# One-hots of the filled tiles in a two-layer graph network: made by distance and ramp on ScalarE instead of by comparison on VectorE

## What is computed

```python
edge_index = jnp.stack([src, dst])
h = jnp.maximum(_layernorm(x, axis=-1), 0.0)
x = x + _L0_gnn_ref(h, edge_index, W, b)          # xw[src] * norm, summed by dst
h = jnp.maximum(_layernorm(x, axis=-1), 0.0)
x = x + _L1_gnn_ref(h, edge_index, ...)           # attention over the edges:
q = (h[src] @ Wq.T + bq).reshape(-1, 8, 16)
k = (h[dst] @ Wk.T + bk).reshape(-1, 8, 16)
v = (h[dst] @ Wv.T + bv).reshape(-1, 8, 16)
exp_att = jnp.exp(jnp.clip(einsum('ehd,ehd->eh', q, k) / 4, -10, 10))
out = segment_sum(exp_att / segment_sum(exp_att, src)[src] * v, src)
out = layernorm(out + h) * gamma + beta
```

## Time and profile before

| | us |
|---|---|
| median of 3 runs | 2204.95 |
| lowest, highest | 2202.63, 2205.7 |
| the profiled execution, its own time | 2208.58 |
| its span, first to last instruction | 2206.9 |
| granted TensorE clock, mean of the span | 0.886 of full |

### The profile page before, as it was taken

One profiled execution on the slowest core, in us unless ns is written; L12 is line 12 of the kernel. 1 busy time (PEld: TensorE's weight loads), 2 busy tenths in 40 slices (PEclk: granted clock), 3 DMA queues, 4 the chain that ended last, 5 costly groups with the idle time before them and its releaser, 6 DMA issues. The chain is left out here.

```text
span 2206.9 us, 44517 instructions
## 1 busy us (share of the span) xinstructions
PE 1621.2 (73%) x10081; PEld 1279.8 (58%) x10082; DVE 1861.9 (84%) x5001; ACT 1295.7 (59%) x3546; POOL 1495.3 (68%) x1570
## 2 busy tenths in 40 slices
PE   5524355887787787868877778888888888888880
PEld 4424343555554555545556567777777777777770
DVE  9998998967676787676686679999999999999996
ACT  8744446967677767677775544444444444444443
POOL 0067777777777777777773467777777777777756
PEclk8866667988898888989889889999999999999995
DMA  4031221111111111121110744445454454445443
GB/s 140 17 84 52 53 53 51 52 51 52 52 51 52 52 53 52 52 52 51 52 53 14 230 137 137 140 137 142 137 138 142 136 140 139 140 136 140 138 114 58
DMA packets 123938, 202.72 MB, mean 92 GB/s; under 512 B 34205, under 2 KB 85789, under 8 KB 123781
## 3 DMA queue, kind: packets, MB, share of 16 engines
q0 software_dynamic: 59984, 143.85, 23.4%
q1 hardware_dynamic: 54037, 50.75, 8.3%
q10 hardware_dynamic: 9888, 7.80, 1.7%
HBM read 183.20 MB, written 19.08 MB: 92 GB/s over the span
## 5 line engine op out<-in xcount | busy, mean ns | idle before, releaser
L303 POOL DMA_INDIRECT rows<-y_tab,idx x832 | 798.0, 959 | 308.2 <-issue 307.0
L1364 POOL DMA_INDIRECT x<-kv_tab,kv_idx x648 | 625.9, 966 | 263.0 <-issue 179.2
L783 ACT ACTIVATE sort_v<-sort_t,staged,minus 128x128 f16<-128x128 f16 x914 | 360.7, 480 | 115.0 <-PE ps_sort L875 113.3
L622 DVE TENSOR_SCALAR sort_v<-iota_h,staged 128x128 f16<-128x128 f16 x748 | 249.5, 334 | 162.4 <-PE ps_sort L875 161.9
L875 PE MATMUL ps_sort<-sort_hi,sort_v 128*128 128x496 f16 x1662 | 360.2, 374 | 0.1
L833 PE MATMUL ps_sum<-rows,hot 128*128 128x128 f32 x1664 | 254.3, 318 | 139.7 <-DMA rows<-y_tab,idx 97.1
L1614 PE MATMUL ps_kv<-kv_s,hot_low 128*128 x1314 | 325.8, 384 | 31.6 <-DVE hot_low L1388 30.9
L833 PEld LDWEIGHTS ps_sum<-rows,hot 128*128 128x128 f32 x1664 | 246.2, 233 | 152.9 <-issue 75.6
L1601 PE MATMUL ps_m<-msg,x 128*128 128x136 f32 x1728 | 251.6, 288 | 97.3 <-DVE msg L1416 96.7
L1601 PEld LDWEIGHTS ps_m<-msg,x 128*128 128x128 f32 x1728 | 214.5, 189 | 177.4 <-issue 177.4
L775 ACT ACTIVATE sort_t<-iota_h,minus 128x128 f16<-128x128 f16 x831 | 250.9, 387 | 104.1 <-DVE minus L614 104.1
(11 more groups left out here) (293 smaller groups left out, 2170.9 us busy)
## 6 DMA issues: line engine op xcount, KB each, us to landing
weights<-src_tab SPq DMA_DIRECT2D x219, 128.0 KB
rows<-y_tab,idx POOLq DMA_INDIRECT x832, 2.5
x<-kv_tab,kv_idx POOLq DMA_INDIRECT x648
weights<-low_tab ACTq DMA_DIRECT2D x56, 128.0 KB
kv_tab<-kv_s SPq DMA_DIRECT2D x12, 512.0 KB
x<-x_in SPq DMA_DIRECT2D x1, 3328.0 KB, 13.1
out<-x SPq DMA_DIRECT2D x12, 256.0 KB
out<-h POOLq DMA_DIRECT2D x12, 256.0 KB, 7.6
```

The source lines that it names most:

```text
L303: pool.indirect_dma_start(out=rows[:, k * SPAN + n, :], out_offset=None, in_=y_tab, in_offset=bass.IndirectOffsetOnAxis(ap=idx[:, k, n:n + ...
L622: nc.vector.tensor_scalar(sort_v2[:, k % 2, m, :], iota_h[:, 0:P], staged[:, LO, c:c + 1], staged[:, V2, c:c + 1], ALU.is_equal, ALU.mult)
L783: last = nc.scalar.activation(to[:, k % 2, m, :], sort_t[:, k % 2, m, :], ACT.Relu, bias=staged[:, v, c:c + 1], scale=minus[:, v, c:c + 1])
L1364: pool.indirect_dma_start(out=rows[:, u, k, :], out_offset=None, in_=kv_tab, in_offset=bass.IndirectOffsetOnAxis(ap=idx[:, u, k:k + 1], ax ...
```

## The change

`hots_of_low` leaves VectorE. ScalarE makes the same values in two steps, as it does for `src`: `low_distances` writes |place - own lane - 128 w| into `hot_low` (Abs with a bias), and `hots_of_low` turns it in place into relu(1 - distance). Each step works on one **half** (`pair`, two tiles, 256 columns) with three instructions, one for each window. In a pass ScalarE does: quad 0 distances of half 0, quad 1 ramp of half 0, quad 2 distances of half 1, quad 3 ramp of half 1, each placed right before the wait for `clip_done`. Each ramp is followed by the load of its half of `from_low` for the next pass (two loads of half the size, where there was one). `lanes` becomes the negative of what it was, as it is a bias now. TensorE's `fill` waits for `hot_low_ready` at tiles 0 and 2. `clip_done` becomes one semaphore instead of four, counted through.

```diff
 
-            def load_low(engine, i):
+            def load_low(engine, i, pair):
 
-                lanes_of_quad = low_tab[ds(i * QUAD, QUAD), :].rearrange("k d -> (k d)")
-                engine.dma_start(from_low, lanes_of_quad.unsqueeze(0).to_broadcast([P, QUAD * P])).then_inc(low_in, 16)
+                lanes_of_pair = low_tab[ds(i * QUAD + 2 * pair, 2), :].rearrange("k d -> (k d)")
+                engine.dma_start(from_low[:, pair * 2 * P:(pair + 1) * 2 * P],
+                                 lanes_of_pair.unsqueeze(0).to_broadcast([P, 2 * P])).then_inc(low_in[pair], 16)
 
...
 
-                def hots_of_low(i):
-
-                    v.wait_ge(low_in, (i + 1) * 16)
-                    v.wait_ge(fill_done, i * QUAD)
-                    for w in range(WINDOWS):
-                        last = nc.vector.tensor_scalar(hot_low[:, w, :], from_low, lanes[:, w:w + 1], None, ALU.is_equal)
-                    last.then_inc(hot_low_ready, 1)
-
                 def products(i, u):
...
                     nc.vector.tensor_scalar(attc[:, u % 2, :], att, -40.0, 40.0, ALU.max, ALU.min)\
-                        .then_inc(clip_done[u], 1)
+                        .then_inc(clip_done, 1)
 
...
                     one_hot(i if u < 2 else i + 1, (u + 2) % QUADS)
-                    if u == 2:
-                        hots_of_low(i + 1)
                     scores(i, u)
...
                 nc.vector.tensor_scalar(minus_lane[:, :], lane[:, :], -1.0, -1.0, ALU.mult, ALU.add).then_inc(lane_set, 1)
+                nc.vector.tensor_scalar(lanes[:, :], iota[:, 0:WINDOWS], -float(P), lane[:, :], ALU.mult, ALU.subtract).then_inc(lane_set, 1)
                 then(nc.vector.tensor_copy(columns_from_1, iota[:, 1:P + 1]))
-                then(nc.vector.tensor_scalar(lanes[:, :], iota[:, 0:WINDOWS], float(P), lane[:, :], ALU.mult, ALU.add))
-                v.wait_ge(low_in, 16)
-                for w in range(WINDOWS):
-                    last = nc.vector.tensor_scalar(hot_low[:, w, :], from_low, lanes[:, w:w + 1], None, ALU.is_equal)
-                last.then_inc(hot_low_ready, 1)
                 one_hot(0, 0)
...
                     add_sums(end, 3, k, buckets[QUAD + k])
-                v.wait_ge(low_in, (end + 3) * 16)
-                v.nop(nofuse=True)
 
...
 
-                load_low(act, 0)
+                def low_distances(i, pair):
+
+                    act.wait_ge(low_in[pair], i * 16 + 16)
+                    if not (isinstance(i, int) and i == 0):
+                        act.wait_ge(fill_done, i * QUAD - QUAD + pair * 2 + 2)
+                    part = slice(pair * 2 * P, (pair + 1) * 2 * P)
+                    for w in range(WINDOWS):
+                        last = nc.scalar.activation(hot_low[:, w, part], from_low[:, part], ACT.Abs, bias=lanes[:, w:w + 1])
+                    last.then_inc(low_off, 1)
+
+                def hots_of_low(i, pair):
+
+                    act.wait_ge(low_off, i * 2 + pair + 1)
+                    part = slice(pair * 2 * P, (pair + 1) * 2 * P)
+                    for w in range(WINDOWS):
+                        last = nc.scalar.activation(hot_low[:, w, part], hot_low[:, w, part], ACT.Relu, bias=1.0, scale=-1.0)
+                    last.then_inc(hot_low_ready, 1)
+                    load_low(act, i + 1, pair)
+
+                for pair in range(2):
+                    load_low(act, 0, pair)
                 for u in range(QUADS - 1):
                     set_idx(0, u)
 
                 nc.scalar.activation(warm[:, :], ones[:, 0:1], ACT.Exp)
-                act.wait_ge(hot_low_ready, 1)
-                load_low(act, 1)
-                act.wait_ge(lane_set, 1)
+                act.wait_ge(lane_set, 2)
+                for pair in range(2):
+                    low_distances(0, pair)
+                    hots_of_low(0, pair)
                 for u in range(2):
...
                             copy_filled(i, 1)
+                        if u % 2 == 0:
+                            low_distances(i + 1, u // 2)
+                        else:
+                            hots_of_low(i + 1, u // 2)
 
-                        act.wait_ge(clip_done[u], i + 1)
+                        act.wait_ge(clip_done, i * QUADS + u + 1)
                         nc.scalar.activation(exps, attc[:, u % 2, :], ACT.Exp, scale=0.25).then_inc(w_ready[u], 1)
...
                         distance(i if u < 1 else i + 1, (u + 3) % QUADS)
-                        if u == QUADS - 1:
-                            act.wait_ge(hot_low_ready, i + 2)
-                            load_low(act, i + 2)
                     copy_filled(i + 1, 0)
+                passes = passes_of(mybir.EngineType.Activation)
+                for pair in range(2):
+                    wait_positive(act, low_in[pair], passes * 16 + 32)
+                act.nop(nofuse=True)
 
...
                                              skip_runtime_bounds_check_because="the chip takes the minimum of it and of this bound")
-                    if k == 0:
-                        pe.wait_ge(hot_low_ready, i + 1)
+                    if k % 2 == 0:
+                        pe.wait_ge(hot_low_ready, i * 2 + 1 + k // 2)
                     if k % 2 == 0 and not (isinstance(i, int) and i == 0 and k == 0):
```

More of the change, by code:

```diff
@@ L1316, in build @@
             prod_done, clip_done, w_ready, msg_ready, sum_done, acc_done = (
-                per_quad("prod_done"), per_quad("clip_done"), per_quad("w_ready"), per_quad("msg_ready"),
+                per_quad("prod_done"), sem("clip_done"), per_quad("w_ready"), per_quad("msg_ready"),
                 per_quad("sum_done"), per_quad("acc_done"))
@@ L1320, in build @@
             tile_added = sem("tile_added")
-            low_in, hot_low_ready, fill_done, filled = (
-                sem("low_in"), sem("hot_low_ready"), sem("fill_done"), sem("filled"))
+            low_in, low_off, hot_low_ready, fill_done, filled = (
+                [sem(f"low_in{n}") for n in range(2)], sem("low_off"), sem("hot_low_ready"), sem("fill_done"), sem("filled"))
             def of_pass(engine, i, part):
```

## The result

| | before | after |
|---|---|---|
| median of 4 runs each, us | 2204.06 | 2171.52 |
| lowest, highest | 2202.63, 2205.7 | 2170.63, 2173.06 |
| profiled execution, its own time | 2208.58 | 2171.95 |
| its span | 2206.9 | 2170.3 |
| granted clock, mean of the span | 0.886 | 0.886 |

The ratio is 0.9853, 95% interval 0.9836 to 0.987: 32.5 us faster. The forecast was 2151.3 us with a range of 2146 to 2176. The sign and the range held, but of a gain of 53.7 us only 60% came. The interesting part is the 20 us between forecast and result.

What follows compares the result with a forecast made beforehand. VectorE was taken as the bound, GpSimd next at 15.0 us a pass: 52.3 us from entry and passes plus 1.4 us behind them, 53.7 us off 2208.6, leave 2154.9; less 3.6 for the median, 2151.3 us, range 2146 to 2176.

Steps and rivals of the forecast that it cites:

- stretched gathers: Rival, GpSimd in the second layer's passes: gathers stay at their mean, 15.3 us a pass, 2167 us; chance 0.11.
- late exp: Rival, ScalarE's exp behind the new activations: VectorE stalls, about 15.5 us a pass, 2178 us; chance 0.14.
- What bounded the kernel, VectorE with the comparisons: Second layer's edge work: VectorE, 95.4% busy, sets 16.06 us a pass, three comparisons costing 1.41 us of it.
- VectorE's new floor of 14.65 to 14.7 us: VectorE's pass without comparisons: 16.06 - 1.41 = 14.65 us, or four quads of 3.68 us, 14.7 us.
- GpSimd late next at 12 x 1.25 = 15.0 us: GpSimd becomes the bound: twelve gathers 1.25 us apart make 15.0 us a pass, above VectorE's 14.7.
- ScalarE's twelve activations: New 256-column activations, 0.48 and 0.40 us each, add 4.0 us a pass; ScalarE reaches 11.6 us of 15.
- The exp behind them, nothing: The exp queued behind the new activations costs VectorE nothing, with 0.5 us to spare.
- ScalarE as the bound: Rival: half-width activations cost as much as full ones, 16.8 us a pass on ScalarE, 2251 us; chance 0.04.
- The entry, 4.2 us later: Start of the second layer: distances and ramps before the loop and first exp move the first `values` by 4.2 us.
- The loads are asked for three quads ahead and hidden: ScalarE's loads of `from_low` for the next pass are issued three quads ahead and cost no time.
- rows 2.2 us after their gather: Gathered rows land 2.2 us after their gather's end, putting the last quad 2's `products` at 2088.8 us.
- The tail: Behind the last quad 2's `products`, one more set of comparisons is gone, saving 1.4 us.

Runs made afterwards that it cites:

- h1: The changed kernel without the loads of from_low inside the loop (stale one-hots): 2150.14 us against 2205.5 us for the kernel before, one run each.

## Why the prediction was right, and where it was wrong

The sign follows from the mechanism that was forecast. That the time lies in the range doesn't: the range reached up to 2176 us for stretched gathers and a late exp, neither came, and what did come, late rows, had no term in it. In that the range held by luck.

**What bounded the kernel, VectorE with the comparisons: right.** They went, and the quad that held them fell from 5.03 to 3.97 us.

**VectorE's new floor of 14.65 to 14.7 us: wrong by 0.3 us.** The prediction took four quads of 3.68 us. The loop's turn costs 0.27 us on top when nothing covers it (0.86 against 0.59 us), which makes 14.97 us. It subtracted the comparisons whole, though 0.27 of their 1.41 us lay over the turn. In h1 that cost next to nothing, since GpSimd's 15.0 us is as much, but the third of a microsecond of slack that VectorE was to have was not there. What it costs in the changed kernel, where late rows could be caught up with, no run shows.

**GpSimd late next at 12 x 1.25 = 15.0 us: the size right, the bound only in part.** h1 runs at 14.997 us, but VectorE's own 14.97 us would make as much of it within 0.03 us, and its `products` wait for rows 0.3 us in 800, not 0.3 us a pass. That the forecast of the pass fits h1 so closely is in this respect luck: two floors, one of them mis-sized, met. The rival of stretched gathers (15.3 us) falls: the mean is 945 ns. In the kernel before, 105 gathers after 1290 us ran beside comparisons, 67 of these took 1.06 to 1.19 us, and no other took more than 1.0 us; now none does. The Trainium skill (SBUF — State Buffer, Who interferes with whom) has it that a `tensor_scalar` of VectorE in a two-port mode shuts out descriptor writing for gathers; the trace agrees in so far as the comparisons are gone and the gathers of 1.15 us with them, while no run shows the mode.

**ScalarE's twelve activations: right in what counts, the sizes good.** Estimated 480 and 400 ns, measured 496 and 400 ns; three in a row put the next start 1.2 and 0.9 us on, against 1.1 and 0.9 us. ScalarE is 76% busy, 11.8 us of a pass of 15.4, against 11.6 us forecast. The Trainium skill's rule that was weighed there (VectorE: DVE Perf Modes, The TRN2 errata) gives an estimate of 400 ns for both kinds, which is the measured value for the ramps and 0.1 us short for the distances. The Trainium skill (ScalarE: Activation LUTs, What ACT_TABLE_LOAD costs) also gives 280 ns with a pointer bias and 186 ns without, plus 0.833 ns a column, an estimate of 493 and 399 ns at 256 columns; the trace agrees with it in both.

**The exp behind them, nothing: right.** It starts at 1716.18 right behind the distances, and VectorE waits for an exp 2.4 us in all in 800 us, in passes 4, 20 and 44 only (of which below). The rival of a late exp and the one of ScalarE as the bound fall.

**The entry, 4.2 us later: the direction right, 2.7 us measured.** From the first gather to the first gather of pass 1 it is 18.17 us (1268.69 to 1286.86), 15.46 before.

**"The loads are asked for three quads ahead and hidden", and rows 2.2 us after their gather: this step failed.** It looked at when the loads have to be there, and they are. It didn't ask whom they run into: the change makes two of one load and places one of them beside the last gathers of a group. The landing of 2.2 us was taken from the first layer, where rows are half as long. In the second layer of the changed kernel `products` start 3.8 to 4.9 us (1331.58 to 1336.44) after the gather in every fourth pass, while 2.3 us were enough in h1. The trace of the kernel before would have shown 1.9 us in the mean and up to 3.1 us in every fourth pass. In the kernel before, `products` of quad 2 started 3.9 us after the last gather's end (0.83 us ahead of 1704.18 in the earlier trace rows, that is 1703.35, to 1707.21 in the earlier trace rows), in other passes up to 4.3 us. That is slack which the shorter pass used up, and the load of half 0, now beside the last gather, came on top.

The size of it, by quads, changed kernel against h1: ahead of quad 2's `products` 4.011 against 3.685 us, 0.33 us a pass and 17.3 us over 53 passes; quad 0 3.726 against 3.672 us, 2.9 us; the other two together 1.2 us. The sum is 0.40 us a pass, 21.4 us. (The two kernels may have run on different chips.) Against the forecast end of the passes, 2088.8 us, that gives 2110.2; less 1.5 us of the entry and 3.5 us that all began earlier it is 2105.2, measured 2105.39 us. The tail returned 1.0 instead of 1.4 us. That leaves the profiled execution 17.0 us above its forecast of 2154.9, and the median 20.2 us above 2151.3, because the profiled execution lay 3.6 us over the median before and 0.4 us after.

What of quad 0? **Windows of 2 us, after, behind the late rows of pass 3** (columns as above):

```profile
1340.00:1342.00 2.00, 1.38 (x8) 1.41 (x9) 2.00 (x5) 1.55 (x4) 1.39 (x3) 0.78 0.48 121
1342.00:1344.00 2.00, 2.00 (x11) 2.00 (x10) 1.81 (x7) 0.96 (x3) 1.70 (x2) 0.50 0.72 183
1344.00:1346.00 2.00, 2.00 (x11) 1.76 (x11) 2.00 (x5) 0.34 (x1) 1.39 (x3) 0.86 0.44 109
```

**Timeline of the same place:**

```profile
1336.44 0.69 DVE L1391 TENSOR_TENSOR by_tile<-ps_q,x 128x512 f32<-128x512 f32 x1 [1.41 <-DMA x<-kv_tab,kv_idx]
...
1340.62 1.67 PE L1612 MATMUL ps_m<-msg,x 128*128 128x136 f32 x8 [2.10 <-DVE msg L1409]
...
1342.08 1.91 PE L1600 MATMUL ps_q<-q,by_tile 128*128 x8
...
1345.66 0.60 ACT L1512 ACTIVATE x<-ps_kv 128x512 f32<-128x512 f32 x1 [2.09 <-PE ps_kv L1625]
```

After the late `products` TensorE gets its messages late and idles 2.10 us ahead of its `sums`. The granted clock then is 0.78, 0.50 and 0.86 in three windows: in the middle one 1.2 GHz, the lower of its two levels, for the whole 2 us, and in the two others for part of the time. `sums` takes 1.67 us instead of 1.17, `expand` of eight matmuls 1.91 instead of 1.05 us, and `copy_filled` comes 2.09 us late. It is so in passes 4, 20 and 44, which take 16.1 us each. That the idle time brings the clock down was not tried alone; h1 has no such idle time, and none of its windows of 100 us up to 2000 is below 1.00.

**What the prediction said would be seen**: no gather of 1.15 us, no wait for `hot_low`, activations near 480 and 400 ns, VectorE busy 92% (91.7% in the mean of 1300 to 2100 us) came. `products` 15.0 us apart and almost no wait of GpSimd for `values` (28 times, 25.7 us) didn't. `distance(0, 0)`, forecast near 1279, is at 1275.01; with the 3.5 us that all began earlier that is 1278.5, half a microsecond short. VectorE was to wait 0.3 us a pass for rows, evenly; it waits 15.6 us in 52 passes, which is 0.3 us in the mean, but in lumps, most of them of over a microsecond. An even wait is slack in the faster engine and free; a lump in an engine that is as slow as the bound is lost. The same busy share stood for another thing.

## What to carry to other kernels

When a change takes work off the bounding engine, list for every transfer not only when it has to be there but what it runs beside: a small load next to the last gather of a group can hold up data that had slack only as long as the kernel was slower. Two engines with equal floors have no slack between them, so each single late event is paid in full and comes back as a wait on the other. And take from the removed work what it covered: here a loop's turn cost nothing behind 1.4 us of comparisons, and 0.27 us without them.

## What was not expected of the hardware

- A load of 64 KB beside gathers and a 128 KB load: gathers' packets in 3.2 us fall from 106 to 37 and the total from 146 to 77 GB/s, but only in every fourth pass, though the load is issued at nearly the same moment in the two before it. The kernel before shows the same passes, by 0.5 us in the mean; h1 doesn't.
- Idle times of TensorE of 2.10 and 2.19 us (at 1340.62 and 1586.74) were followed by matmuls at 1.2 GHz for some 3.4 us, those of 2.06 and 2.13 us (1710.51 and 1772.24) by none at all, `sums` taking 1.17 us behind them.
- Chips differ by 30% for this kernel: 2203 to 2206 us on those of the result and of h1, and medians of 2835 to 2861 us on four others, where engines stop for microseconds at a time without a visible wait and the granted clock is 0.79 in the mean. One and the same kernel, the one without loads, is 2.5% faster than the kernel before on the one kind and 5% to 6% slower on the other.
